# Spreading the reciprocals of a linear attention's denominators over the channels through DRAM instead of on TensorE

## What is computed

```
q, k, v = split(x @ Wqkv.T + b)              # 16 heads of 32 channels
q = elu(q * scale) + 1;  k = elu(k * scale) + 1
k_cumsum, kv_cumsum = cumsum(k), cumsum(k * v)     # over the tokens
denom = clip(sum over the head's 32 channels of q * k_cumsum, EPS)
y = q * kv_cumsum / denom                    # one denominator for a head and a token
x = layernorm(x + y @ Wproj.T + bproj)
```

## Time and profile before

| what | value |
|---|---|
| time, median of 3 runs | 2354.44 us (2353.5 to 2355.1) |
| the profiled execution: its span | 2352.2 us |
| PE busy | 2332.6 us, 99% of the span, 12060 matmuls |
| DVE busy | 1652.7 us, 70% |
| ACT busy | 1144.1 us, 49% |
| POOL busy | 451.6 us, 19% |
| DMA | 354.77 MB, mean 151 GB/s |

### The profile page before, as it was taken

How to read it: one execution, slowest core, us unless ns; L and a number is a source line. 1 busy time by engine, 2 the same in 40 slices (tenths; PEclk the granted TensorE clock), 3 DMA queues, 4 the chain that set the end, 5 groups by cost and what they waited for, 6 DMA issues and landing times.

```text
span 2352.2 us, 34307 instructions
## 1 busy us (share of the span) xinstructions
PE 2332.6 (99%) x12060; PEld 1927.6 (82%) x12060; DVE 1652.7 (70%) x2863; ACT 1144.1 (49%) x1902; POOL 451.6 (19%) x395
## 2 busy tenths in 40 slices
PE   9999999999999999999999999999999999999998
PEld 7878888888888888888888888888888888888787
DVE  8886685866858668586675867758677586875643
ACT  5354445454454544545455444545454454554543
POOL 1112211121121212212122111211113111121200
PEclk9999999999999999999999999999999999999999
DMA  9255445463444634446354454544536435453332
GB/s 341 83 160 188 117 144 163 133 218 106 150 155 143 207 102 179 132 144 206 108 182 133 138 193 126 187 127 143 180 117 206 117 135 179 126 161 99 100 116 90
DMA packets 97276, 354.77 MB, mean 151 GB/s; under 512 B 11858, under 2 KB 11986, under 8 KB 86994
## 3 DMA queue, kind: packets, MB, share of 16 engines
q1 hardware_dynamic: 80210, 319.02, 38.2%
q0 software_dynamic: 16896, 33.56, 9.0%
HBM read 329.47 MB, written 23.07 MB: 150 GB/s over the span
## 4 chain that ended last, share of the span: by engine, by line
PE 92%; DVE 1%; ACT 1%; issue 1%; POOL 0%; DMA 0%; SPq 0%; POOLq 0%; DVEq 0%; ACTq 0%
PE acc L1274 29%; PE m L1049 13%; PE h_ps L1250 10%; PE h_ps L1252 10%; PE h_ps L1251 10%; PE m L1079 6%; PE m L1133 2%; PE m L1210 2%; PE m L1117 2%; PE m L1118 2%; PE m L1119 2%; PE m L1231 1%; PE m L1090 1%; PE m L1103 1%; PE acc L1290 0%
## 5 line engine op out<-in xcount | busy, mean ns | idle before, releaser
L561 ACT ACTIVATE hid<-h_ps,b 128x512 f32<-128x512 f32 x252 | 173.6, 689 | 598.2 <-PE h_ps L1252 597.5
L1049 PE MATMUL m<-xT_hi,wq 128*128 128x512 f32 x1320 | 408.2, 390 | 0.3 <-DVE xT_lo L1010 0.3
L1250 PE MATMUL h_ps<-x2T_hi,we_hi 128*128 128x512 f32 x1008 | 400.4, 397 | 2.4 <-DVE x2T_lo L905 2.4
L1274 PE MATMUL acc<-we_hi,h_hi 128*128 128x512 f32 x1008 | 400.8, 398 | 1.5 <-DVE h_lo L921 1.5
L921 DVE TENSOR_TENSOR h_lo<-hid,h_hi 128x512 fp32r<-128x512 f32 x252 | 224.3, 890 | 252.9 <-ACT h_hi L568 252.9
L1252 PE MATMUL h_ps<-x2T_hi,we_lo 128*128 128x512 f32 x1008 | 392.9, 390 | 0.0
L1274 PE MATMUL acc<-we_hi,h_lo 128*128 128x512 f32 x1008 | 392.8, 390 | 0.0
L1274 PE MATMUL acc<-we_lo,h_hi 128*128 128x512 f32 x1008 | 392.7, 390 | 0.0
L1251 PE MATMUL h_ps<-x2T_lo,we_hi 128*128 128x512 f32 x1008 | 392.4, 389 | 0.0
L911 DVE TENSOR_TENSOR we_lo<-raw,we_hi 128x1024 fp32r<-128x1024 f32 x256 | 319.9, 1250 | 31.2 <-ACT we_hi L551 31.2
L499 ACT ACTIVATE e_f<-m,sb_qkv,scale 128x512 f32<-128x512 f32 x116 | 90.5, 780 | 479.8 <-PE m L1079 477.7
(11 more groups left out here) (259 smaller groups left out, 3368.6 us busy)
## 6 DMA issues: line engine op xcount, KB each, us to landing
raw<-in_w SPq DMA_DIRECT2D x256, 512.0 KB, 4.2
wq<-wq_scratch SPq DMA_DIRECT2D x168, 512.0 KB, 3.3
x<-in_x_tok SPq DMA_DIRECT2D x16, 1024.0 KB, 5.5
x<-in_b_proj POOLq DMA_DIRECT2D x16, 1024.0 KB, 14.7
ctx_T<-in_ctxT SPq DMA_DIRECT2D x16, 1024.0 KB, 8.2
x<-in_b POOLq DMA_DIRECT2D x16, 1024.0 KB, 11.8
ctx_tok<-in_ctx_tok SPq DMA_DIRECT2D x15, 1024.0 KB, 4.7
out_dram<-x SPq DMA_DIRECT2D x15, 1024.0 KB, 4.8
```

The costliest lines, as they stand in the source:

```text
L561: act.activation(hid[:, f % 2, :], up_bank(b, f)[:, :], ACT.Relu, bias=b1[:, b % 2, f:f + 1]).then_inc(h_done, 1)
L1049: pe.matmul(bank(a, j)[:, :], w[:, s, t, :], x_hi[:, t, :], start=(t == 0 and s == 0), stop=False)
L1250: pe.matmul(ps, we_hi[:, g % NW, js], x2T_hi[:, j, :], start=(j == 0), stop=False)
L1274: last = pe.matmul(acc[t][:, :], hx[:, f % 2, ts], wx[:, g % NW, C:], start=(f == 0 and n == 0), stop=(f == FC - 1 and n == 2))
```

## The change

From batch 2 on (`ON_PE = 2`) the four spread matmuls are left out. DVE stops after the reciprocal. ACT issues in slot 20 (`RALL`) four stores of the 16 rows of each segment to a DRAM tensor `rden_scratch`, which then has heads by tokens; in slot 21 it waits for all four stores and issues four loads, each of which brings four heads' rows, repeated 32 times, to 128 partitions of `xT_lo`, whose old content is no longer used. DVE waits for two loads at a time and multiplies from there. The low part of y later overwrites the same place.

So that a load can repeat a block of four rows, the channels of 128 are reordered on the host (in Wqkv, bqkv and Wproj) such that the head is the innermost index: partition p belongs to head p mod 4 of its tile. `head_sum` is accordingly made from a small matrix `fourth`, a reduction of the identity on DVE and four copies on POOL at the start, in place of two mask operations. Batches 0 and 1 still use the matmuls. The slots of batches 3 to 15 become those that batch 2 had: SPREAD 22 (21 before), HIGH 23 (22), LOW 25 (23), PROJECT 26 (25), CTX_SUM 27 (26), SPLIT_X 30 (29), NORM_1 32 (31).

```diff
-SPREAD = plan(21, 20, 21, 22)
-HIGH = plan(22, 20, 21, 23)
-LOW = plan(23, 21, 23, 25)
-PROJECT = plan(25, 23, 25, 26)
-CTX_SUM = plan(26, 25, 26, 27)
-SPLIT_X = plan(29, 28, -6, 30)
-NORM_1 = plan(31, 29, 30, 32)
+SPREAD = plan(22, 20, 21)
+HIGH = plan(23, 20, 21)
+LOW = plan(25, 21, 23)
+PROJECT = plan(26, 23, 25)
+CTX_SUM = plan(27, 25, 26)
+SPLIT_X = plan(30, 28, -6)
+NORM_1 = plan(32, 29, 30)
...
+        def spread_rows(a, cc):
+            return rden_dram[a, XH * cc:XH * cc + XH, :].unsqueeze(0).broadcast_to([HD, XH, T])
...
-                if (a := at(i, h, RALL)) is not None:
+                if (a := at(i, h, RALL)) is not None and a >= ON_PE:
+                    act.wait_ge(rden_done, a + 1 + 2 * ON_PE)
+                    for s in range(TT):
+                        act.dma_start(rden_dram[a, :, s * P:s * P + P], rden[s * SEG:s * SEG + NH, :]).then_inc(rden_st, 16)
+                if (a := at(i, h, RALL + 1)) is not None and a >= ON_PE:
+                    act.wait_ge(rden_st, 16 * TT * (a - ON_PE + 1))
+                    for n in range(2):
+                        for cc in range(2 * n, 2 * n + 2):
+                            act.dma_start(y_lo(a)[:, cc, :].bitcast(F32),
+                                          spread_rows(a, cc)).then_inc(rden_in[n], 16)
+                if (a := at(i, h, RALL)) is not None and a < ON_PE:
...
                 dve.reciprocal(rden[:, :], den[:, :].bitcast(F32)).then_inc(rden_done, 1)
+                if a >= ON_PE:
+                    return
...
             def times_reciprocal(a, cc):
-                dve.wait_ge(rb_mm, CC * a + cc + 1)
+                if a < ON_PE:
+                    dve.wait_ge(rb_mm, CC * a + cc + 1)
+                else:
+                    dve.wait_ge(rden_in[cc // 2], 32 * (a - ON_PE + 1))
                 dve.wait_ge(num_done, CC * a + cc + 1)
-                dve.tensor_tensor(numer(a)[:, cc, :], numer(a)[:, cc, :], AB[(cc + 1) % 2][:, :], ALU.mult).then_inc(y_done, 1)
+                rb = AB[(cc + 1) % 2][:, :] if a < ON_PE else y_lo(a)[:, cc, :].bitcast(F32)
+                dve.tensor_tensor(numer(a)[:, cc, :], numer(a)[:, cc, :], rb, ALU.mult).then_inc(y_done, 1)
...
+            dve.wait_ge(made, 7)
+            dve.reduce_sum(fourth[:, :], ident[:, :].rearrange("p (d l) -> p l d", l=XH), AX.X).then_inc(fourth_done, 1)
...
                 for n in range(2):
-                    if (a := at(i, h, SPREAD + n)) is not None:
+                    if (a := at(i, h, SPREAD + n)) is not None and a < ON_PE:
                         spread_reciprocal(a, 2 * n)
                         spread_reciprocal(a, 2 * n + 1)
```

More of the change, by code:

```diff
@@ L39 @@
 LAST = FC - 4
+ON_PE = 2
 def upto(batch, per, n):
@@ L101, in build @@
     wq_dram = nc.dram_tensor("wq_scratch", [JOBS, P, 2 * CC * P], F32, kind="Internal").ap()
+    rden_dram = nc.dram_tensor("rden_scratch", [NB, NH, T], F32, kind="Internal").ap()
     with ExitStack() as ctx:
@@ L137, in build @@
         ident, ones, ones_r = sb("ident", [P, P]), sb("ones", [P, P]), sb("ones_r", [P, P], F32R)
-        head_sum = sb("head_sum", [P, CC, SEG])
+        head_sum, fourth = sb("head_sum", [P, CC, SEG]), sb("fourth", [P, XH])
         den, rden = sb("den", [P, P], F32R), sb("rden", [P, P])
@@ L169, in build @@
         mean_ps, route_ps = M2[:, 0:P], M2[0:1, 0:NE]
+        fourth_done = sem("fourth_done")
         made, masks_done, preset, heads_mm = sem("made"), sem("masks_done"), sem("preset"), sem("heads_mm")
@@ L184, in build @@
         kvc_done, q_done, qk_done, num_done = sem("kvc_done"), sem("q_done"), sem("qk_done"), sem("num_done")
+        rden_st, rden_in = sem("rden_st"), [sem("rden_in0"), sem("rden_in1")]
         den_mm, den_max, rden_done, rall_done, rb_mm = (sem(n) for n in ("den_mm", "den_max", "rden_done", "rall_done", "rb_mm"))
@@ L266, in build @@
         block = ctx.enter_context(nc.Block())
-        MADE = 11
+        MADE = 13
         head_ps = H_PS[:, :].rearrange("p (t c) -> p t c", t=CC)
@@ L372, in _ @@
                 pool.memset(m[:, :], value).then_inc(made, 1)
-            pool.memset(head_sum[:, :, :], 1.0).then_inc(made, 1)
+            pool.memset(head_sum[:, :, :], 0.0).then_inc(made, 1)
             pool.memset(zeros, 0.0).then_inc(made, 1)
-            twice = head_sum[:, :, :].rearrange("p t (r h) -> p t r h", r=2)
             masks = [(ident[:, :], ALU.not_equal, 1.0, 0, [[-1, P]], 1),
-                     (twice, ALU.is_ge, 0.0, 0, [[P, CC], [0, 2], [-HD, NH]], 1),
-                     (twice, ALU.is_ge, 0.0, HD - 1, [[-P, CC], [0, 2], [HD, NH]], -1),
                      (low_set[:, :], ALU.is_ge, 0.0, -NH, [[-SEG, TT]], 1),
@@ L384, in _ @@
                                    channel_multiplier=step_p).then_inc(made, 1)
+            pool.wait_ge(fourth_done, 1)
+            for cc in range(CC):
+                pool.tensor_copy(head_sum[:, cc, :].rearrange("p (r h) -> p r h", r=2)[:, :, XH * cc:XH * cc + XH],
+                                 fourth[:, :].unsqueeze(1).broadcast_to([P, 2, XH])).then_inc(made, 1)
             pool.wait_ge(made, MADE)
@@ L733, in denominator @@
                 dve.wait_ge(den_mm, a + 1)
-                if (due := upto(a - 1, TT, TT)) is not None:
-                    dve.wait_ge(rall_done, due)
+                if 0 < a <= ON_PE:
+                    dve.wait_ge(rall_done, TT * a)
+                elif a > ON_PE:
+                    dve.wait_ge(rden_st, 16 * TT * (a - ON_PE))
                 dve.tensor_scalar(den[:, :].bitcast(F32), den_ps, EPS_DEN, None, ALU.max).then_inc(den_max, 1)
@@ L1107, in project @@
                     pe.wait_ge(wplo_done, 1)
-                if t < 2:
+                if t < 2 and a < ON_PE:
                     pe.wait_ge(y_done, CC * a + 3 + t)
-                else:
+                elif t >= 2:
                     pe.wait_ge(res1_done, TT * a + t - 1)
@@ L1382 @@
                ("wqg", "bqg", "wkg", "bkg", "wvg", "bvg", "wql", "bql", "wkl", "bkl", "wvl", "bvl", "wp", "bp")}
-    wq, wk, wv = np.split(g["L0_attn_Wqkv"], 3, axis=0)
+    order = np.arange(C).reshape(CC, XH, HD).transpose(0, 2, 1).reshape(-1)
+    wq, wk, wv = (w[order] for w in np.split(g["L0_attn_Wqkv"], 3, axis=0))
     w1 = g["L0_ffn_W1"].reshape(NE, CC, P, FC, P).transpose(0, 3, 2, 1, 4).reshape(NE, FC, P, C)
@@ L1392 @@
                            for w in (wk, wv, wq)], axis=1).reshape(JOBS, P, CC * P),
-        "w_proj": weights(g["L0_attn_Wproj"]).reshape(P, CC * C),
-        "b_qkv": column(g["L0_attn_bqkv"]),
+        "w_proj": weights(g["L0_attn_Wproj"][:, order]).reshape(P, CC * C),
+        "b_qkv": column(g["L0_attn_bqkv"].reshape(3, C)[:, order]),
         "scale": g["L0_attn_scale"].reshape(1, 1),
```

## The result

The changed kernel is slower. Its median is 2388.18 us (2383.85 to 2390.59, four runs) beside 2354.44 us for the kernel before on the same chip; the ratio is 1.0143 with a 95% interval of 1.0128 to 1.0157. A fourth run of the kernel before took 8350.22 us and isn't counted in these two numbers. The forecast was 2345.4 us in a range of 2339.5 to 2358: wrong in sign, and outside the range. The profiled execution took 2383.85 us with a span of 2382.2 us.

A forecast was written before the change was run, and what follows sets the result against it. PE was taken to bound the kernel, busy 99% and waiting for nobody from batch 2 to the last batch's attention. 2354.4 - 12.9 (removed matmuls) + 3.9 (stalls) = 2345.4 us, range 2339.5 to 2358.

The forecast's parts named there:

- Removed matmuls: Four spread matmuls a batch on PE, 0.92 us, gone in batches 2 to 15: 12.9 us saved.
- The bound of 375.8: Batch 3: latest landing of the first two reciprocal loads before PE's UP matmuls in slot 24 must wait.
- T0 = 376.1: Batch 3: landing of the first two loads, 5.0 us after 371.06; PE stalls 0.3 us a batch, 3.9 altogether.
- rival (b): Loads squeezed between SP's and POOL's transfers land late; each microsecond past 375.8 costs 13 us, up to 2366.2; chance 0.14.
- The later plan: Batches 3 to 15 take batch 2's slots; counted at nothing, between -1.25 and +1 us, in batch 15.
- the disturbed case: DVE products reading SBUF alone take up to 1.67 us instead of 0.69, putting the bound up to 2 us earlier.
- 56 matmuls fewer: Sign of a right forecast: PE runs 56 matmuls fewer.
- A DVE wait for the reciprocals' DMA: Sign of a right forecast: DVE waits for these loads in nearly every batch, 1 to 4 us each.
- UP waiting some twelve times: Sign on PE: UP matmuls wait for the weight remainder, about 0.3 us each if right, over 1 us for rival (b).
- ACT's held split: Sign of a wrong forecast: UP waits for a remainder ACT's split held up, DMA issues costing ACT over 0.46 us.

The follow-up runs named there:

- old_rows: The changed kernel, but from batch 3 on the loads fetch the previous batch's rows and wait only for that batch's stores; 2387.97 us, ratio 1.0144.
- xt_late: The changed kernel with the 1 MB load of the next xT in slot 24 instead of 20; 2363.83 us, ratio 1.0043.
- x_early: The changed kernel with x loaded in slot 15 instead of 17 from batch 3 on, POOL's bias load behind it in slot 16; 2361.43 us, ratio 1.0032.
- x_early_xt_late: The changed kernel with x loaded in slot 15, the bias in slot 16 and the next xT in slot 24; 2349.96 us, ratio 0.9985.
- reorder_only: The kernel before with only the new channel order and new head matrix; old plan, all batches spread by matmul; 2354.30 us, ratio 1.0001.

## Why the prediction was wrong

**Removed matmuls: right.** 0.9 us a batch, shown where the transfers are left out.

**The bound of 375.8: right.** The sum over batches 3 to 14 of T0 - 12.95 is 26.2 us in the kernel after; PE's waits there, both rows of slot 24 and the five of x_sum (ahead in the same batches, so they use up part of the stall), are 11.8 + 8.8 + 6.8 - 1.5 = 25.9. For old_rows it is 30.1 against 30.0, for xt_late 10.3 against 11.1, for x_early 8.5 against 9.4, for x_early_xt_late 0.1 against 0.2. DVE's pace behind the landing, read from the earlier trace rows, held in these batches: the first two products take 1.29 us. In batch 2 it didn't (below).

**T0 = 376.1: this is the step that failed.** Forecast 13.2 us, measured 15.1. A stall of 0.3 us a batch became 2.2, and 3.9 us of cost became 26. In its terms: the stores took 5.8 us, not 2.2, which is outside the bounds of 1.5 to 3.6 taken from the earlier trace rows. Those rows are of loads at another place, with another queue around them. A store was counted as small, so cheap; it is small, but it is not alone in the DMA engines. Only in batch 15, with nothing beside it, did it take the 1.4 to 1.5 us of the lower bound.

In the mean the last store was issued 4.8 us behind the denominators, earlier than the 5.5 counted, as ACT's sequencer was ahead of the weight split that starts at 367.05; but all four had landed only at 11.2 (7.7 counted). The second load was issued at 11.8, 3.6 us later than counted, and took 3.4 us, not 5.0. This error in the other direction is luck: old_rows shows that loads issued early, at 7.5, take 6.6. The right question was not "how long does this DMA take" but "when is the queue empty", and the bytes to be added to the earlier trace rows were 1 MB of loads on DMA engines already at a share of 1.03. The 0.60 of the next window was read as room; with the added 1 MB it was 0.92.

This was rival (b), given 0.14. Its price of 13 us for each microsecond was right in kind: 2.2 us a batch over its twelve batches, 26.2 us, on 2341.5 gives 2367.7. The reason against it, that the engines aren't full from 374, was read from the trace without the change.

The Trainium skill's rule in "DMA: Bandwidth & Descriptors", "Queues, rings and completion order", turns between queues packet by packet, was cited as speaking against the change and given no term. The runs fit it, though none shows the turns themselves: the same 8 KB takes 5.8, 4.7, 2.4 and 1.5 us as neighbours go. The formula of the Trainium skill in "DMA: Bandwidth & Descriptors", "Anatomy of one DMA", fitted there on DMAs of GpSimd, gives 2.6 us for one load, an estimate; by it there would be no stall. That is near the best here, 2.8, and far off the 6.6 of the crowd.

**The later plan: mis-sized.** Taken at nothing (-1.25 to +1), it costs 3.9 - 1.25 = 2.65 us plus the clock below; together 4.35; alone it was 4.3 us (2358.35 - 2354.07). The slip: the earlier trace rows was read on ACT and PE, and POOL's queue, where the shift is made and which the moved step passes with a DMA issue, was left out.

**Not foreseen: the clock.** The granted clock of PE in a window of the kernel after, behind the 2.54 us wait of batch 2 (the third number from the end):

```profile
243.00:246.00 3.00, 2.78 (x7) 2.23 (x8) 3.00 (x5) 1.83 (x3) 0.00 (x0) 0.50 0.49 173
246.20:248.00 1.80, 1.80 (x15) 1.06 (x15) 0.00 (x0) 0.38 (x1) 0.00 (x0) 1.00 0.00 0
```

At 0.50, the lower level of 1.2 GHz, PE loses half the time. The kernel after has five such stretches that before has not, 1.7 us lost in each if half of it is counted as lost (from 242.73, 532.86, 1119.95, 1560.28 and 2184.91), each at the end of or behind a wait, or a pair of waits in one slot, of 1.75 to 3.91 us together; counted so, with the start and the end, they cost 14.4 us against 6.4, so 8 us more. Not every such wait has one: behind the pairs of batches 10 and 12, 1.95 and 2.07 us, the clock stays at the upper level.

**The sum again.** 2354.4 - 12.9 + 26.2 (T0) + 2.5 (batch 2, L1278) + 2.65 (tail) + 8.0 (clock) + 2.3 (a later start: the denominators of batch 1 at 110.38 instead of 108.11) = 2383.2, measured 2383.85 in the profiled execution. On the spans the same terms lead from 2352.2 to 2381.0, measured 2382.2. The profiled execution is the fastest of the four; the median is 4.3 us higher, and no trace shows where that lies. The start differs from trace to trace, 107.5 to 112.4, and isn't the change's: reorder_only, which has it too, is at 108.70 and no slower in its median. Batch 2's wait stays in all kernels with the transfers, with T0 at 13.1 as well. PE is at that batch's UP after 14.9 us already, not after 15.6, and the first two products are slower. DVE and POOL in x_early_xt_late, then in the kernel before:

```profile
236.72 2.79 DVE L775 TENSOR_TENSOR ctx_tok<-ctx_tok,xT_lo 128x512 f32<-128x512 f32 x2 [4.29 <-DMA xT_lo<-rden_scratch]
235.98 2.98 POOL L419 TENSOR_TENSOR x_sum<-x_sum,x 128x512 f32<-128x512 f32 x2
```

```profile
236.92 1.27 DVE L749 TENSOR_TENSOR ctx_tok<-ctx_tok,m 128x512 f32<-128x512 f32 x2
235.99 3.96 POOL L411 TENSOR_TENSOR x_sum<-x_sum,x 128x512 f32<-128x512 f32 x2
```

POOL adds up x beside them. The products of before, which read one operand from a PSUM bank, don't mind; the new ones, which read SBUF alone, do. Over the nine kernels with transfers this pair takes 1.73 to 3.01 us where POOL's additions overlap it by 0.58 to 2.38 us, and in the other batches, with no overlap, 1.29. It is the disturbed case that the prediction named for the products and set aside; for batches 3 to 14 that was right, for batch 2 not.

**The signs named beforehand.** 56 matmuls fewer: seen. A DVE wait for the reciprocals' DMA in nearly every batch: seen, but longer. UP waiting some twelve times: seen, at 1.0 us behind another wait, 1.4 us together in batch 3 and more in most others, the sign for (b). ACT's issues: the loads' stand 0.62 us apart (2.50 for four), the stores' 0.44, against the 0.46 counted; ACT's held split wasn't what came last.

## What to carry to other kernels

A transfer that replaces work on the critical engine has to be costed in the queue it joins: add its bytes to the windows in which it runs; where the share nears 1, as here, what it takes alone is no price for it, whatever its own size. Before such a change move the large transfers that nobody waits for out of the way; here that turned a ratio of 1.0143 into 0.9985, and 0.9968 with the last batch left on matmuls, though the same shifts were worth nothing by themselves. A step moved in one engine's order has to be followed to every engine that feeds it, in the last batch too. And a transfer moved to a later slot comes there only if its engine waits for something there: the bias did not, and the kernel became 2.7% slower than before.

## What the runs showed of the hardware

- A store of 16 pieces of 512 bytes lands after 1.4 to 1.5 us in a free queue, and after 5.8 us (median, up to 7.2) beside two 1 MB transfers at a DMA share of about 1.
- A wait can cost more than itself: at or behind five of them (1.75 to 3.91 us) PE ran at 1.2 GHz for a while, with some 1.7 us more lost each time; behind two of 1.95 and 2.07 us it didn't.
- ACT's sequencer issues DMAs while its engine still works on earlier instructions: in batch 3 of the kernel after the first store is issued at 371.76, and the engine is at the normalisation until 372.64 (its last tile starts at 371.84 and takes 0.80).
- Four matmuls fewer a batch move the instruction fetches. Five new waits of 0.7 to 1.2 us on POOL's sums came with that, which even the kernel without any transfer has; that the one makes the other is read from their coincidence, not shown.
- Two DVE products that read SBUF alone take 1.29 us, and up to 3.01 us beside POOL's additions in SBUF; two that read one operand from PSUM take 1.27 beside them.
